# One preparation per step, shared operand forms and a wide reciprocal in the first of two attentions

## The chip, the core and the metric

The kernel runs on one core of a Trainium2 chip. Its time is the device time in microseconds (us), the median of several runs. A profiled execution of the same program gives the trace: TensorE (PE) for matrix products, with its weight loads (PEld) listed apart, VectorE (DVE), ScalarE (ACT), GpSimd (POOL) and the queue of SyncE (SP), which issues loads.

## The reference

Two layers on `x` of 128 x 64 x 128 (batch, rows, features), each a cross attention to a context of 128 x 64 x 96 and a mixture of experts. The change lies in the first attention alone:

```python
q = (x @ wq + bq).reshape(B, Sq, H, D).transpose(0, 2, 1, 3)      # x is layer-normalised; 16 heads of 8
k = (y @ wk + bk).reshape(B, -1, H, D).transpose(0, 2, 1, 3)
v = (y @ wv + bv).reshape(B, -1, H, D).transpose(0, 2, 1, 3)
scores = jnp.einsum('bhqd,bhkd->bhqk', q, k) / jnp.sqrt(D)
attn = jax.nn.softmax(scores, axis=-1)
out = jnp.einsum('bhqk,bhkd->bhqd', attn, v)
x = x + jnp.tanh(g_xattn[0]) * (out.transpose(0, 2, 1, 3).reshape(B, Sq, E) @ wo + bo)
```

After it come the first mixture, the second attention and the second mixture, which sorts rows by expert and gathers them again.

## The kernel before

`attention_of_layer0` works on 64 tiles of 128 rows, two batches in each. Four tiles are a group (`GT`), so there are 16 groups. The phase is a software pipeline written out by hand: in step t every engine works on several tiles at once, in the order of its own `step` function, and semaphores join the engines. The loop `loop_steps` runs eight steps (two groups, `u` from 0 to 7) in each iteration.

What happens to tile n, by step:
- step n: TensorE makes the scores of all 16 heads (L663, 32 rows by 64 columns of the array at a time) in one of two pairs of PSUM banks. VectorE takes the negated maximum of each head (L412) and splits it into two bf16 parts (cast L423, difference L425). TensorE transposes the parts (L737, called R in what follows) into the bank `small`.
- step n+1: ACT has copied them to `rows` (L602). TensorE adds them to the scores (the subtraction, L673), ACT takes exponentials (L571).
- step n+2: VectorE sums them for each head (L409, `denom`), takes the reciprocal (L418, 16 elements a partition) and spreads it over the 8 places of each head (L430, 16 to 128 elements). TensorE transposes the probabilities in two halves (L690); ACT copies each half (L578).
- step n+3: TensorE transposes the spread reciprocals (L706) and multiplies probabilities and values (L719, strips of 32 columns), both into `pv`. ACT copies the product (L591, `heads_raw`), VectorE multiplies by the reciprocals (L443, called heads).
- step n+4: TensorE applies the output weights (L686, y, into the bank `small`), VectorE adds y to X (L436, the X update).

VectorE's order in a step is sum (n+2), maximum (n), reciprocal (n+2), cast and parts (n), wide copy (n+2), X update (n+4), heads (n+3). After heads come, in three of a group's four steps, the statistics of a later group (L375, L379), `offset` (L385) and `v_odd` (L393, half of the copies of values). R of step t waits, besides the parts, for the X update of the same step, since y and the transposed parts share a bank:

```python
if tile_now(t, 4) is not None:
    pe.wait_ge(x_updated, t - 3)
pe.transpose(rows_ps, parts[:], c.ident_bf[:]).then_inc(rows_mm, 1)
```

Each group also needs four preparations in the one bank `prep`, in the order KEYS, ROWS (transposes of the normalised rows, L633), QUERIES and VALUES. For group g they are made in the steps of group g-1: KEYS and ROWS in the first step, KEYS between subtraction and y, ROWS and the others behind the values product, QUERIES in the second, VALUES in the third, none in the fourth. Keys and queries are made with 64 columns of weights at a time (L638), values in the same way (L644). ACT copies the results out (`evacuate`). GpSimd multiplies `kT` by four masks (`spread_k`, L494) into one of two `k_heads`, in the second step of the group, takes the power -1/2 of the variance (L70, L72) and adds the output bias to X (L485).

## Time and profile before

| | |
|---|---|
| median of 3 runs | 909.94 us (908.78 to 912.01) |
| profiled execution | 908.92 us, its span 907.1 us, granted TensorE clock 0.959 of full |
| busy in the whole span | PE 777.2 us, PEld 600.7, DVE 690.6, ACT 568.8, POOL 469.1 |
| first attention (to about 321 us), stretch 202.00 to 238.40 | 36.40 us: PE 35.77, PEld 23.93, DVE 33.00, ACT 28.02, POOL 17.49; clock 1.00 |

Busy times are those of a profile: matmuls are pipelined and their ends are modelled, so the distance from one start to the next says more than the duration. The two numbers behind a form such as 32*64 are the rows and columns of the array that an operand uses. The records of an fp32 product are two for each matmul.

### The profile page before, as it was taken

Reading aid. Unit: us, or ns where it says so; the run is one execution under the profiler, and the core shown is the slowest. Engines: PE = TensorE matmul, PEld = TensorE weight load, DVE = VectorE, ACT = ScalarE, POOL = GpSimd, SP = SyncE. Lnnn points to the kernel's source line nnn. Section 1 sums busy time; section 2 is a strip of 40 time slices with the busy share of each in tenths; the row PEclk is TensorE's granted clock in tenths of the full one; section 3 lists DMA queues with packets and bytes.
Section 4 is the critical chain, followed back from the end, with each engine's and each line's share of the span. In section 5 each row is a group of like instructions: output and inputs, shape, how many; then the busy total and the mean of one; then the engine's idle time right before and its main releaser. Section 6 shows DMA issues by size and latency. Waiting matters only on the chain. (4 is left out here: it accounts for less than half of the span.)

```text
span 907.1 us, 26462 instructions
## 1 busy us (share of the span) xinstructions
PE 777.2 (86%) x8408; PEld 600.7 (66%) x8408; DVE 690.6 (76%) x2993; ACT 568.8 (63%) x1209; POOL 469.1 (52%) x505
## 2 busy tenths in 40 slices
PE   4999999999999889998998987876887888888870
PEld 2566666666666557676676665766787777788870
DVE  3989889888998968888887877455676565668764
ACT  3777777777777566878888775354354454455430
POOL 3554445444555012377777766645555555555560
PEclk9999999999999989999999999688899999999995
DMA  9101000010000020011111111311223322246638
GB/s 243 43 23 43 20 20 20 27 34 20 20 20 2 3 59 10 13 51 46 42 52 45 49 45 40 89 49 49 68 78 86 90 70 79 76 122 171 176 91 280
DMA packets 62329, 58.12 MB, mean 64 GB/s; under 512 B 10327, under 2 KB 52216, under 8 KB 62232
## 3 DMA queue, kind: packets, MB, share of 16 engines
q1 hardware_dynamic: 44664, 34.42, 14.3%
q0 software_dynamic: 8640, 17.84, 5.7%
q10 hardware_dynamic: 8928, 4.70, 1.8%
q8 instruction: 45, 0.74, 0.3%
q14 instruction: 52, 0.43, 0.2%
HBM read 32.91 MB, written 24.02 MB: 63 GB/s over the span
## 5 line engine op out<-in xcount | busy, mean ns | idle before, releaser
L1132 POOL DMA_INDIRECT contributions<-v_heads,d_token x142 | 137.9, 971 | 105.6 <-PE bc_bank L1882 67.9
L1863 PE MATMUL bc_bank<-d_xT,d_w 128*128 128x128 f32 x1136 | 161.6, 287 | 35.6 <-DVE d_xT L1381 30.1
L1863 PEld LDWEIGHTS bc_bank<-d_xT,d_w 128*128 128x128 f32 x1136 | 143.0, 197 | 46.1 <-DVE d_xT L1381 37.6
L1116 POOL DMA_INDIRECT sorted_rows<-r_send,r_slots x128 | 126.7, 990 | 47.3 <-issue 40.3
L1640 ACT ACTIVATE b_hidden<-bc_bank 128x256 f32<-128x256 f32 x142 | 54.5, 384 | 143.8 <-PE bc_bank L1863 126.5
L494 POOL TENSOR_SCALAR a_k_heads<-a_kT,first 128x512 f32<-128x512 f32 x60 | 93.1, 1569 | 0.8 <-ACT a_kT L547 0.8
L1634 ACT COPY d_w<-w 128x512 f32 x142 | 87.1, 614 | 4.2 <-issue 1.9
L412 DVE TENSOR_REDUCE a_neg_max<-a_scores 128x16 f32<-128x1024 f32 x64 | 78.1, 1221 | 8.1 <-PE a_scores L663 6.9
L571 ACT ACTIVATE a_probs<-a_scores 128x1024 f32<-128x1024 f32 x64 | 65.6, 1025 | 29.5 <-PE a_scores L673 29.4
L578 ACT COPY a_probsT<-a_probsT_bank 128x512 f32<-128x512 f32 x128 | 74.8, 584 | 13.4 <-PE a_probsT_bank L690 12.8
L690 PE MATMUL a_probsT_bank<-first,a_probs 128*128 128x128 f32 x512 | 79.7, 278 | 2.2 <-ACT a_probsT L578 0.3
L409 DVE TENSOR_REDUCE a_denom<-a_probs 128x16 f32<-128x1024 f32 x64 | 77.3, 1209 | 1.7 <-issue 1.3
L663 PE MATMUL a_scores<-a_k_heads,a_qT 32*64 32x256 f32 x1024 | 70.8, 391 | 3.0 <-issue 2.7
L1376 DVE TENSOR_TENSOR b_hidden<-b_hidden,bc_bank 128x256 f32<-128x256 f32 x72 | 29.9, 416 | 53.6 <-ACT b_hidden L1640 20.5
L690 PEld LDWEIGHTS a_probsT_bank<-first,a_probs 128*128 128x128 f32 x512 | 57.7, 141 | 12.5 <-issue 5.8
L485 POOL TENSOR_TENSOR X<-X,out_bias 128x512 f32 (+1 forms) x16 | 20.3, 1269 | 87.6 <-ACT a_xn L534 84.9
L1709 PE MATMUL bc_bank<-b_xnT,w 128*128 128x512 f32 x96 | 50.3, 636 | 12.8 <-ACT c_kT L1559 7.5
L1376 DVE TENSOR_TENSOR b_weighted<-b_hidden,bc_bank 128x256 f32<-128x256 f32 x70 | 29.1, 416 | 34.5 <-PE bc_bank L1882 20.2
L1873 PE MATMUL bc_bank<-first,d_rows 128*128 128x128 f32 x142 | 39.7, 279 | 11.8 <-DVE d_xT L1381 7.5
L1392 DVE TENSOR_SCALAR v_heads<-bc_bank,d_ends 128x128 f32<-128x128 f32 x142 | 48.7, 343 | 1.0 <-PE bc_bank L1882 1.0
L1760 PE MATMUL bc_bank<-w,b_weighted 128*128 128x128 f32 x384 | 46.8, 278 | 0.1
L1398 DVE COPY w_in<-w 128x256 f32 x142 | 46.5, 328 | 0.2
(213 smaller groups left out, 1894.1 us busy)
## 6 DMA issues: line engine op xcount, KB each, us to landing
d_rows<-sorted_rows SPq DMA_DIRECT2D x142, 65.0 KB
X<-in_x SPq DMA_DIRECT2D x16, 256.0 KB, 3.1
b_hidden<-contributions SPq DMA_DIRECT2D x8, 512.0 KB
b_weighted<-contributions SPq DMA_DIRECT2D x8, 512.0 KB
out_x<-X ACTq DMA_DIRECT2D x16, 256.0 KB
ctxT<-in_ctx_T SPq DMA_DIRECT2D x16, 192.0 KB, 3.0
c_ctxT<-in_ctx_T SPq DMA_DIRECT2D x16, 192.0 KB
contributions<-v_heads,d_token POOLq DMA_INDIRECT x142
```

The lines of the kernel that those rows point to most:

```text
L409: dve.reduce_sum(denom[:], probs[u % 2][:].rearrange("p (h k) -> p h k", k=S), AX_X).then_inc(sum_done, 1)
L412: dve.tensor_reduce(neg_max[:], scores[u % 2][:].rearrange("p a (h k) -> p (a h) k", k=S), AX_X, ALU.max, negate=True).then_inc(max_done, 1)
L494: last = pool.tensor_scalar(keys_of_head(par, j), kT[:], c.head_of_group[:, j:j + 1], None, ALU.mult)
L571: act.activation(probs[(u + 1) % 2][:], scores[(u + 1) % 2][:].rearrange("p a n -> p (a n)"), ACT.Exp, scale=SCALE0).then_inc(exp_done, 1)
L578: act.copy(probsT[u % 2][:, half * HU // 2:(half + 1) * HU // 2, :].rearrange("p u q -> p (u q)"), probsT_bank[:]).then_inc(pT_ev, 1)
L663: last = pe.matmul(scores[u % 2][S * b:S * b + S, s, bass.ts(h, 4 * S)], qT[par][rows_in, h, tile, :], k_heads[par][rows_in, tile, h].rear ...
L690: last = pe.transpose(probsT_bank[:, bass.ts(k, P)], probs[u % 2][:, bass.ts(half * HU // 2 + k, P)], c.ident[:])
L1116: pool.indirect_dma_start(dispatch.rows, bass.IndirectOffsetOnAxis(ap=slots[n % 2][:, k, j:j + 1], axis=0), send[n % 2][k][:, j, :], None) ...
L1132: pool.indirect_dma_start(dispatch.contributions, bass.IndirectOffsetOnAxis(ap=token[:, t % KEEP:t % KEEP + 1], axis=0), shares[t % KEEP], ...
L1376: dve.tensor_tensor(d_hidden[m % 4].rearrange("p k n -> p (k n)"), silu[m % 2], uv[m % 2][:, KH * P:2 * KH * P], ALU.mult).then_inc(h_read ...
L1634: act.copy(w12[t % 3][:], c.w12[:, bass.ds(experts[t % 4], 1)].rearrange("d a i h -> d (a i h)")).then_inc(w12_ready, 1)
L1863: last = pe.matmul(uv[m % 2][:, bass.ts(i, P)], w12[m % 3][:, bass.ts(i, P)], xT[m % 4][:], start=True, stop=True)
```

## The change

The diff does four things.
- Operand forms: keys, queries and values are made with strips of 32 columns, four at a time, and the subtraction in pieces of 64 columns.
- Preparations: KEYS goes to the fourth step of a group (`PREP_AT`), for the group after the next one, behind the values product; `preparations` lists them for TensorE and ACT. In step 0 the keys of group 1 are made as well.
- GpSimd: the four masks are spread over three steps (`SPREAD_AT`), the bias is added a step earlier and for a group nearer, behind the first mask, and `later_zeros` is issued in step 62.
- VectorE: L418 is gone; at the place of L430 stands one reciprocal with 128 results a partition, which reads `denom` spread over 8 places. The semaphore `rec_done` goes with it.

```diff
@@ -300,7 +300,6 @@
     probs = [sb(f"a_probs{i}", [P, H * S], F32) for i in range(2)]
     probsT = [sb(f"a_probsT{i}", [P, HU, P], F32) for i in range(2)]
     denom = sb("a_denom", [P, H], F32)
-    rec = sb("a_rec", [P, H], F32)
     wide_rec = [sb(f"a_wide_rec{i}", [P, H, DH], F32) for i in range(2)]
     heads_raw = sb("a_heads_raw", [P, P], F32)
     heads_outT = sb("a_heads_outT", [P, P], F32)
@@ -320,7 +319,7 @@
     prep_mm, prep_ev, v_odd_ev = sem("a_prep_mm"), sem("a_prep_ev"), sem("a_v_odd_ev")
     k_heads_ready = sem("a_k_heads")
     scores_mm, max_done, part1_done, parts_ready = sem("a_scores_mm"), sem("a_max"), sem("a_part1"), sem("a_parts")
-    sum_done, rec_done, raw_ready = sem("a_sum"), sem("a_rec_done"), sem("a_raw_ready")
+    sum_done, raw_ready = sem("a_sum"), sem("a_raw_ready")
     wide_rec_ready = sem("a_wide_rec")
     rows_mm, rows_ready, sub_mm, exp_done = sem("a_rows_mm"), sem("a_rows_ready"), sem("a_sub_mm"), sem("a_exp")
     pT_mm, pT_ev = sem("a_pT_mm"), sem("a_pT_ev")
@@ -328,8 +327,9 @@
     y_mm, x_updated = sem("a_y_mm"), sem("a_x_updated")
     PREP = 4
     KEYS, ROWS, QUERIES, VALUES = range(PREP)
-    PREP_AT = ((ROWS,), (QUERIES,), (VALUES,), ())
+    PREP_AT = ((ROWS,), (QUERIES,), (VALUES,), (KEYS,))
     NORMALISE_AT = ((), (0,), (1,), (2, 3))
+    SPREAD_AT = ((0,), (1, 2), (3,), ())
     LAST = TILES + 4
 
     def keys_of_head(par, j):
@@ -348,6 +348,12 @@
     def group_at(g0, more):
 
         return None if static(g0) and g0 + more >= G else g0 + more
+
+    def preparations(t, u, g0):
+
+        first = [(1, KEYS)] if static(t) and t == 0 else []
+        parts = first + [(2 if k == KEYS else 1, k) for k in PREP_AT[u % GT]]
+        return [(group_at(g0, more), (u // GT + more) % 2, k) for more, k in parts if group_at(g0, more) is not None]
 
     with nc.Block() as block:
         @block.sync
@@ -405,17 +411,12 @@
                 if m is not None:
                     dve.wait_ge(exp_done, m + 1)
                     if not static(m) or m >= 1:
-                        dve.wait_ge(rec_done, m)
+                        dve.wait_ge(wide_rec_ready, m)
                     dve.reduce_sum(denom[:], probs[u % 2][:].rearrange("p (h k) -> p h k", k=S), AX_X).then_inc(sum_done, 1)
                 if n is not None:
                     dve.wait_ge(scores_mm, n + 1)
                     dve.tensor_reduce(neg_max[:], scores[u % 2][:].rearrange("p a (h k) -> p (a h) k", k=S), AX_X,
                                       ALU.max, negate=True).then_inc(max_done, 1)
-                if m is not None:
-                    dve.wait_ge(sum_done, m + 1)
-                    if not static(m) or m >= 1:
-                        dve.wait_ge(wide_rec_ready, m)
-                    dve.reciprocal(rec[:], denom[:]).then_inc(rec_done, 1)
                 if n is not None:
                     if not static(n) or n >= 1:
                         dve.wait_ge(rows_mm, n)
@@ -426,8 +427,8 @@
                 if m is not None:
                     if not static(m) or m >= 2:
                         dve.wait_ge(spread_mm, m - 1)
-                    dve.wait_ge(rec_done, m + 1)
-                    dve.tensor_copy(wide_rec[u % 2][:], rec[:].unsqueeze(2).broadcast_to([P, H, DH])).then_inc(wide_rec_ready, 1)
+                    dve.wait_ge(sum_done, m + 1)
+                    dve.reciprocal(wide_rec[u % 2][:], denom[:].unsqueeze(2).broadcast_to([P, H, DH])).then_inc(wide_rec_ready, 1)
                 w = tile_now(t, 4)
                 if w is not None:
                     if u % GT == 0:
@@ -485,26 +486,30 @@
                 pool.tensor_tensor(X[:, bass.ts(g, GT), :], X[:, bass.ts(g, GT), :],
                                    c.out_bias0[:].unsqueeze(1).broadcast_to([P, GT, D]), ALU.add).then_inc(bias_added, 1)
 
-            def spread_k(g, par):
-
-                wait_alone(pool, prep_ev, PREP * g + KEYS + 1)
-                if not static(g) or g >= 2:
-                    wait_alone(pool, scores_mm, GT * (g - 1))
-                for j in range(4):
+            def spread_k(g, par, heads):
+
+                if heads[0] == 0:
+                    wait_alone(pool, prep_ev, PREP * g + KEYS + 1)
+                    if not static(g) or g >= 2:
+                        wait_alone(pool, scores_mm, GT * (g - 1))
+                for j in heads:
                     last = pool.tensor_scalar(keys_of_head(par, j), kT[:],
                                               c.head_of_group[:, j:j + 1], None, ALU.mult)
-                last.then_inc(k_heads_ready, 1)
+                if heads[-1] == 3:
+                    last.then_inc(k_heads_ready, 1)
 
             def step(t, u, g0):
+                if static(t) and t == TILES - 2:
+                    later_zeros(pool, c, dispatch)
                 if u % GT == 0:
                     g = group_at(g0, 2)
                     if g is not None:
                         deviation(g)
-                if u % GT == 1:
+                g = group_at(g0, 1)
+                if g is not None and SPREAD_AT[u % GT]:
+                    spread_k(g, (u // GT + 1) % 2, SPREAD_AT[u % GT])
+                if u % GT == 0 and not (static(t) and t < GT):
                     g = group_at(g0, 1)
-                    if g is not None:
-                        spread_k(g, (u // GT + 1) % 2)
-                    g = group_at(g0, 2)
                     if g is not None:
                         add_bias(g)
 
@@ -519,7 +524,6 @@
             add_bias(0)
             add_bias(1)
             loop_steps(pool, 2 * GT, TILES // (2 * GT) - 2, LAST, step)
-            later_zeros(pool, c, dispatch)
             c.ln.deviation(pool, 0)
             c.ln.offset(pool, 0)
 
@@ -578,9 +582,6 @@
                     act.copy(probsT[u % 2][:, half * HU // 2:(half + 1) * HU // 2, :].rearrange("p u q -> p (u q)"),
                              probsT_bank[:]).then_inc(pT_ev, 1)
 
-                g = group_at(g0, 1)
-                if u % GT == 0 and g is not None:
-                    evacuate(g, (u // GT + 1) % 2, KEYS)
                 if tile_now(t, 2) is not None:
                     keep_transposed(t - 2, 0)
                 n = tile_now(t, 3)
@@ -589,10 +590,8 @@
                     if not static(n) or n >= 1:
                         act.wait_ge(o_ready, n)
                     act.copy(heads_raw[:], pv[:, 0]).then_inc(raw_ready, 1)
-                g = group_at(g0, 1)
-                if g is not None:
-                    for k in PREP_AT[u % GT]:
-                        evacuate(g, (u // GT + 1) % 2, k)
+                for g, par, k in preparations(t, u, g0):
+                    evacuate(g, par, k)
                 if tile_now(t, 2) is not None:
                     keep_transposed(t - 2, 1)
                 if tile_now(t, 0) is not None:
@@ -634,14 +633,16 @@
                 if k in (KEYS, QUERIES):
                     w, src = (c.wk0, ctxT[par]) if k == KEYS else (c.wq0, xnT)
                     for h in range(2):
-                        for odd in range(2):
-                            last = pe.matmul(prep[S * odd:S * odd + S, bass.ts(h, GW // 2)], w[:, bass.ts(h, D // 2)],
+                        for strip in range(4):
+                            odd, s = strip // 2, strip % 2
+                            last = pe.matmul(prep[bass.ts(strip, STRIP), bass.ts(h, GW // 2)], w[:, bass.ts(2 * h + s, STRIP)],
                                              src[:].rearrange("p (t b q) -> p b t q", b=2, q=S)[:, odd],
                                              start=True, stop=True)
                 if k == VALUES:
                     for b in range(GB):
-                        for odd in range(2):
-                            last = pe.matmul(prep[S * odd:S * odd + S, bass.ts(b, D // 2)], ctxT[par][:, bass.ts(b, S)],
+                        for strip in range(4):
+                            odd, s = strip // 2, strip % 2
+                            last = pe.matmul(prep[bass.ts(strip, STRIP), bass.ts(b, D // 2)], ctxT[par][:, bass.ts(2 * b + s, STRIP)],
                                              c.wv0[:].rearrange("p (u h w) -> p h u w", h=2, w=DH)[:, odd],
                                              start=True, stop=True)
                 last.then_inc(prep_mm, 1)
@@ -670,12 +671,10 @@
 
                     pe.wait_ge(rows_ready, n + 1)
                     for s in range(2):
-                        last = pe.matmul(scores[(u + 1) % 2][:, s, :], rows[bass.ts(s, STRIP), :], c.head_cols[bass.ts(s, STRIP), :],
-                                         start=False, stop=True, skip_group_check=True)
+                        for b in range(2):
+                            last = pe.matmul(scores[(u + 1) % 2][bass.ts(b, S), s, :], rows[bass.ts(s, STRIP), bass.ts(b, S)],
+                                             c.head_cols[bass.ts(s, STRIP), :], start=False, stop=True, skip_group_check=True)
                     last.then_inc(sub_mm, 1)
-                g = group_at(g0, 1)
-                if u % GT == 0 and g is not None:
-                    prepare(g, (u // GT + 1) % 2, KEYS)
                 n = tile_now(t, 4)
                 if n is not None:
                     pe.wait_ge(o_ready, n + 1)
@@ -720,10 +719,8 @@
                                                  probsT[(u + 1) % 2][:, k, bass.ts(b, S)], start=(odd == 0 and b == 0),
                                                  stop=(odd == 1), skip_group_check=True)
                     last.then_inc(pv_mm, 1)
-                g = group_at(g0, 1)
-                if g is not None:
-                    for k in PREP_AT[u % GT]:
-                        prepare(g, (u // GT + 1) % 2, k)
+                for g, par, k in preparations(t, u, g0):
+                    prepare(g, par, k)
                 n = tile_now(t, 2)
                 if n is not None:
                     pe.wait_ge(pT_ev, 2 * n + 1)
```

## Rows read from the trace of the kernel before

**Rows 1.** Timeline of DVE, the maxima: start us, us, engine, line
```profile
203.45 1.22 DVE L412 TENSOR_REDUCE a_neg_max<-a_scores 128x16 f32<-128x1024 f32 x1 [0.34 <-PE a_scores L663]
...
213.30 1.21 DVE L412 TENSOR_REDUCE a_neg_max<-a_scores 128x16 f32<-128x1024 f32 x1
...
218.20 1.23 DVE L412 TENSOR_REDUCE a_neg_max<-a_scores 128x16 f32<-128x1024 f32 x1
...
221.70 1.23 DVE L412 TENSOR_REDUCE a_neg_max<-a_scores 128x16 f32<-128x1024 f32 x1
...
227.54 1.21 DVE L412 TENSOR_REDUCE a_neg_max<-a_scores 128x16 f32<-128x1024 f32 x1
...
231.40 1.21 DVE L412 TENSOR_REDUCE a_neg_max<-a_scores 128x16 f32<-128x1024 f32 x1
...
240.26 1.23 DVE L412 TENSOR_REDUCE a_neg_max<-a_scores 128x16 f32<-128x1024 f32 x1 [0.34 <-PE a_scores L663]
```

**Rows 2.** Timeline of PE, a step with keys and rows
```profile
165.48 1.09 PE L663 MATMUL a_scores<-a_k_heads,a_qT 32*64 32x256 f32 x16 [0.48 <-issue]
166.51 0.39 PE L673 MATMUL a_scores<-head_cols,a_rows 32*128 32x512 bf16 x2
166.83 1.08 PE L638 MATMUL a_prep<-ctxT,wkv 96*64 96x256 f32 x8
167.84 0.49 PE L686 MATMUL a_small<-wo,a_heads_outT 128*128 128x128 f32 x2
...
169.39 0.66 PE L633 MATMUL a_prep<-first,a_xn 128*128 128x128 f32 x4
169.88 0.60 PE L690 MATMUL a_probsT_bank<-first,a_probs 128*128 128x128 f32 x4
...
170.47 1.09 PE L663 MATMUL a_scores<-a_k_heads,a_qT 32*64 32x256 f32 x16
```

**Rows 3.** Timeline of DVE and PE, the fourth step of a group
```profile
219.34 0.24 DVE L418 RECIPROCAL a_rec<-a_denom 128x16 f32<-128x16 f32 x1
219.52 0.17 DVE L423 CAST parts<-a_neg_max 128x16 bf16<-128x16 f32 x1
...
219.73 0.17 DVE L425 TENSOR_TENSOR parts<-a_neg_max,parts 128x16 bf16<-128x16 f32 x1
219.83 0.22 DVE L430 COPY a_wide_rec<-a_rec 128x128 f32<-128x128 f32 x1
219.96 0.28 DVE L436 TENSOR_TENSOR X<-a_small,X 128x128 f32 x1
220.16 0.28 DVE L443 TENSOR_TENSOR a_heads_outT<-a_heads_raw,a_pv 128x128 f32<-128x128 f32 x1
220.36 1.21 DVE L409 TENSOR_REDUCE a_denom<-a_probs 128x16 f32<-128x1024 f32 x1
...
220.39 0.22 PE L737 MATMUL a_small<-ident_bf,parts 128*128 128x128 bf16 x1
220.54 1.09 PE L663 MATMUL a_scores<-a_k_heads,a_qT 32*64 32x256 f32 x16
```

**Rows 4.** Timeline of DVE, single operations of the third and first steps
```profile
214.81 0.55 DVE L425 TENSOR_TENSOR parts<-a_neg_max,parts 128x16 bf16<-128x16 f32 x1
...
216.15 0.77 DVE L393 COPY v_heads<-a_prep 64x256 f32<-64x256 f32 x2 [0.25 <-PE a_prep L644]
...
224.94 0.29 DVE L443 TENSOR_TENSOR a_heads_outT<-a_heads_raw,a_pv 128x128 f32<-128x128 f32 x1 [0.80 <-ACT a_heads_raw L591]
```

**Rows 5.** Timeline of POOL, the four masks of one group
```profile
209.99 6.22 POOL L494 TENSOR_SCALAR a_k_heads<-a_kT,first 128x512 f32<-128x512 f32 x4
```

**Rows 6.** Instructions by line: count, ns min/median/max, first and last start, forms
```profile
L212 DVE RECIPROCAL one_over_temp<-temp x1: 157/157/157, 311.4 to 311.4; 128x1 f32<-128x1 f32 x1
...
L1165 DVE RECIPROCAL c_rec<-bc_pair x16: 169/182/183, 361.5 to 610.9; 128x4 f32<-128x4 f32 x16
...
L418 DVE RECIPROCAL a_rec<-a_denom x64: 235/242/253, 31.5 to 316.5; 128x16 f32<-128x16 f32 x64
```

## The prediction

> **What bounds the kernel now.** The page gives TensorE (PE) the most busy time, and in the first attention its records stand end to end, so I read the order of time and not the shares. First I took the starts of VectorE's maximum (L412), one for each of the 64 tiles, which cut this phase into steps [rows 1]. Eight steps take 36.81 us (203.45 to 240.26), so a group of four takes 18.4; the four kinds of step take 4.90, 3.50, 5.84 and 3.86 us. They differ, so each must be asked for its own last wait.
>
> TensorE's own list for the step that prepares keys and rows [rows 2] gives start-to-start times: scores 1.03, subtraction (L673) 0.32, keys 1.01, from y to the end of the values product 1.55, row transposes 0.49, second transposes with the maxima's transpose (R, L737) 0.59: 4.99 us with nothing waited for. Two things are to be seen. Row transposes, four at 128 columns, take 0.49, some 0.11 us each when others follow in one form. The keys' eight records of 256 columns, two side by side in the array, should then take 8 x 0.22 / 2 = 0.87, and take 1.01: about 0.15 us goes at a change of operand form. And TensorE alone needs about 3.5 us for a step without preparation (4.99 less 1.01 and 0.49), 4.5 with the 1.01, and 17.5 for a group, if queries and values cost as much as keys.
>
> The step of 3.50 us shows the other loop [rows 1, 3]. Call the start of the maximum M. The reciprocal (L418) starts at M+1.14, cast at +1.32, parts at +1.53, the wide copy (L430) at +1.63, the X update (L436) at +1.76 and ends at +2.04. R starts 0.15 after that (220.39): it shares the bank `small` with y and waits for `x_updated`. Scores start 0.15 later, and the next maximum 1.16 after them: 2.04 + 0.15 + 0.15 + 1.16 = 3.50, the step to the hundredth. This step is bound by VectorE's small operations between the maximum and X, not by TensorE's 3.49 us of work. Had TensorE been free, VectorE's own order would need 1.96 to heads (L443), 0.20, and 1.13 for the sum (L409): 3.29. The steps of 3.86 and 4.90 are VectorE's too: there come `offset`, or `v_odd` [rows 4], plus collisions with GpSimd's work (the 0.55 us of L425 in rows 4 against 0.17 in rows 3).
>
> Only the step of 5.84 hangs on TensorE: heads (224.94) waited 0.80 us for ACT's copy of `pv` [rows 4], because keys' 1.01 us stands ahead of the values product. Heads start at M+3.24 there instead of M+1.96, and all that follows on VectorE is late by as much.
>
> **TensorE's part of the change.** Scores and subtraction share a form afterwards (32 rows by 64 columns), and so do the values product and each preparation (32-column strips). The preparations have twice the records, four side by side instead of two: the array time stays 0.87. Before, a group changes form 23 times (five in each step and one more each for keys, queries and values); afterwards 16. Seven at 0.15 is 1.05 us, 17 us over 16 groups, if TensorE were what ends last. It then needs 3.35 us for a bare step and 4.2 with a preparation, 16.5 for a group.
>
> **Keys a step ahead.** Keys' matmuls leave the step that is late on `pv` and go behind the values product of the step before. Heads there no longer wait; the 0.80 us goes, up to where VectorE's own order is late (next part). ACT's two copies of keys (L547) move along, to a step with no other evacuation. GpSimd spreads one, two and one heads in three steps and not four at once, and the bias comes a step earlier, between them: the same operations, so the same time on GpSimd, which idles between groups. Keys for the group after next are copied into `kT` only when the spread before them is over. Four heads take 6.2 us [rows 5]; they start in the statistics step, and three steps lie between it and that copy, so even with the bias among them I see no new wait. The DMA loads keep their trigger (values of two groups earlier). `later_zeros` runs straight behind the last spread in either order.
>
> **The wide reciprocal.** L418 on 16 elements and L430 on 128 go; one reciprocal of 128 elements stands at L430's place, between parts and X, which is inside the 3.50 us loop. Its duration D is in no row. Reciprocals took 157 ns for 1 element, a median of 182 for 4 (read from PSUM) and 242 for 16 [rows 6]. That is 5.7 ns an element from 1 to 16, 5.0 from 4 to 16, 8.3 from 1 to 4. Other operations grow far less: cast of 16 elements 0.17, X of 128 elements 0.28, some 1 ns each [rows 3]. Bounds: if 112 more elements streamed at 1 ns, D = 0.242 + 0.11 = 0.35; at 8.3 ns, 0.242 + 0.93 = 1.17. I take the widest span of rows, rounded down a little towards 4 to 16: 5.4 ns, D = 0.85 us.
>
> The Trainium skill, "VectorE: DVE Perf Modes", says that a reciprocal runs as an iterative divide with a repeat count of 8 at 0.96 GHz. Read as 8 cycles an element this is an estimate of 8.3 ns and D = 1.17, and the kernel would end near 942. By this reading 16 elements alone would take 133 of the 242 ns, and the trace speaks against it: that leaves 109 for the rest, where one element takes 157 in all. The duration after decides.
>
> Now M to X. L418 was also a filler: cast needs the maximum, over at M+1.23, and an operation that waits for its predecessor starts 0.04 after its end (parts after cast). So cast moves only from +1.32 to +1.27. Parts +1.48, reciprocal +1.58, X at D less the 0.09 of overlap that L430 shows, +2.34. X was at +1.76: **0.58 us later**.
>
> **The sum, per group.**
> - Plain step: 3.50 becomes 2.34 + 0.28 + 0.15 + 0.15 + 1.16 = 4.08: +0.58. TensorE has slack in it: keys now stand there, but 4.2 is reckoned from its scores, which start early when the `v_odd` step before has delayed only VectorE.
> - `offset` step: on VectorE throughout: +0.58.
> - `v_odd` step: +0.58, less the 0.25 that it waited for values [rows 4], now done in time: +0.33.
> - Statistics step: heads at M+2.54 in place of M+3.24 (`pv` is copied by about M+2.1): -0.70.
>
> Together +0.79 us a group, of 18.4. Fifteen full periods give 11.9 us; start and tail I leave even. The profiled execution took 908.9 us (span 907.1), the median is 909.9: 1.0 apart. So 920.8 against the profiled execution, 921.8, say **922**, against the median. The 17 us saved on TensorE turns into waiting for X.
>
> **Rivals.**
> - *The reciprocal streams* (D near 0.35). Then VectorE needs about the old 3.3 to 3.5 and TensorE ends last: some 17.1 us a group with the waits that remain, 1.3 less, 21 us: 889. The balance tips at D = 0.85 - 0.79/4 = 0.65 us. Below it the kernel is faster. For: doing many elements is what such an engine does cheaply. Against: three rows that rise far more than 1 ns an element. Chance 0.16.
> - *The reciprocal is steeper* (D 0.95 to 1.17): each 0.1 us is 64 x 0.1 = 6.4 us, so 928 to 942. For: the step from 1 to 4. Chance 0.10.
> - *Fewer collisions with GpSimd.* With the spread cut in three and the wide copy gone, the delayed operations (0.38 for L425 in the `v_odd` step, as much around `offset`) may fall between GpSimd's. At most 0.7 a group, 11 us: 911, no change. Against: GpSimd is busy for as long, in the same two steps, and L425 and the cast stay. Chance 0.12.
> - *As summed*: 0.62, with its own range 915 to 928.
>
> **Chances and range.** From 907 to 912.6 (0.3%, which is about what these runs can tell: their own spread is 908.8 to 912.0) nothing would be seen. Slower: the forecast and the steeper case, 0.72. Same: 0.11. Faster: the streaming case and a remnant, 0.17. The range 903 to 935 leaves out the ends at 889 and 942, about 2 in 10.
>
> **What the profile after would show.** A RECIPROCAL writing `a_wide_rec`, 128x128, at 0.85 us (right from 0.80 to 0.90). X starting 2.3 us after the maximum. The plain step at 4.1, the statistics step near 5.2. R waiting for X in most steps and TensorE's busy share in this phase falling. Preparations about 0.87 after the values product, without the 0.15 between. No wait of heads for `pv`. I would be wrong above all through D; next, if R did not wait for X, since then VectorE's sum alone holds (3.87 a plain step) and the loss shrinks by 0.2 us in one step of four.

## The result and the profile after

The changed kernel takes 928.83 us (median of 4 runs, 923.44 to 930.28), the kernel before 909.54 (4 runs, 908.78 to 912.01). The ratio is 1.0196, with a 95% interval of 1.015 to 1.0243: slower by about 2%, 17.8 us by the ratio and 19.3 us between the medians. The forecast was 922, slower, in a range of 903 to 935. Direction and mechanism held; the size was 12 us forecast against 18 by the ratio.

The profiled execution of the changed kernel took 923.4 us, the fastest of the four; its span is 921.6 against 907.1. Two starts cut the span well: the last X update began at 320.2 before and begins at 337.6 now. So the first attention lost 17.4 us, and all behind it took 2.9 us less in this execution (the other three runs, up to 930.3, were not profiled, so what varies there stays open). Inside the first attention, by the starts of the maxima: until the 9th 1.8 us (55.94 to 57.77), in six iterations of the loop 8.0, in the last seven steps 5.9, from the last maximum to the last X update 1.6.

The plain step, the fourth of a group, which took 3.50 us before [rows 1, 3], stands like this in the timeline of VectorE and TensorE of the changed kernel (start us, us, engine, line):

```profile
225.25 1.22 DVE L418 TENSOR_REDUCE a_neg_max<-a_scores 128x16 f32<-128x1024 f32 x1
226.57 0.17 DVE L424 CAST parts<-a_neg_max 128x16 bf16<-128x16 f32 x1
226.78 0.17 DVE L426 TENSOR_TENSOR parts<-a_neg_max,parts 128x16 bf16<-128x16 f32 x1
226.88 0.94 DVE L431 RECIPROCAL a_wide_rec<-a_denom 128x128 f32<-128x128 f32 x1
227.74 0.23 DVE L437 TENSOR_TENSOR X<-a_small,X 128x128 f32 x1
227.88 0.27 DVE L444 TENSOR_TENSOR a_heads_outT<-a_heads_raw,a_pv 128x128 f32<-128x128 f32 x1
228.08 1.21 DVE L415 TENSOR_REDUCE a_denom<-a_probs 128x16 f32<-128x1024 f32 x1
228.11 0.22 PE L734 MATMUL a_small<-ident_bf,parts 128*128 128x128 bf16 x1 [0.49 <-DVE X L437]
...
229.42 1.23 DVE L418 TENSOR_REDUCE a_neg_max<-a_scores 128x16 f32<-128x1024 f32 x1
```

From the maximum to the start of X it is 2.49 us, where it was 1.76; the transpose R (now L734) waits 0.49 us for X by name; 1.68 us after the start of X comes the next maximum. Sum 4.17. In the whole first attention R waits for X in 46 of 64 steps, 26.5 us together. The reciprocal takes 0.946 us in the median. Its row among the instructions by line, to be set beside [rows 6]:

```profile
L431 DVE RECIPROCAL a_wide_rec<-a_denom x64: 937/946/954, 31.9 to 332.7; 128x128 f32<-128x128 f32 x64
```

Busy time in a stretch of one iteration's length (us, then each engine with its number of instructions, the granted clock, DMA share and GB/s) shows the bound moving. TensorE was busy 35.8 of 36.4 us before; here it is 34.8 of 38.2, and VectorE 35.9:

```profile
170.80:209.00 38.20, 34.80 (x712) 23.92 (x712) 35.90 (x79) 28.62 (x63) 17.40 (x14) 1.00 0.08 24
```

In the statistics step, heads no longer wait for `pv` (first line, 2.72 us after a maximum at 210.56, where [rows 4] had 3.24), and in the values step the difference of the parts is short again (second line, 0.55 in [rows 4]):

```profile
213.28 0.27 DVE L444 TENSOR_TENSOR a_heads_outT<-a_heads_raw,a_pv 128x128 f32<-128x128 f32 x1
...
221.79 0.17 DVE L426 TENSOR_TENSOR parts<-a_neg_max,parts 128x16 bf16<-128x16 f32 x1
```

The largest single loss was not in the forecast. Between the 58th and the 59th maximum one cast of 16 elements took 4.15 us, and ended 0.04 us after GpSimd's zeros did. This is the timeline of the changed kernel there:

```profile
291.05 1.23 DVE L418 TENSOR_REDUCE a_neg_max<-a_scores 128x16 f32<-128x1024 f32 x1
292.38 4.15 DVE L424 CAST parts<-a_neg_max 128x16 bf16<-128x16 f32 x1
292.47 0.52 POOL L196 MEMSET probs<- 128x512 f32 x1
...
293.14 3.35 POOL L200 MEMSET fill<- 128x3900 f32 x1
296.56 0.17 DVE L426 TENSOR_TENSOR parts<-a_neg_max,parts 128x16 bf16<-128x16 f32 x1
```

TensorE waited 3.70 us for the X update behind it, and its granted clock was then 0.50 from 298 to 300 us and 0.65 from 300 to 302; in the kernel before it was 1.00 from 24 to 320 us. Before, cast and memset met more luckily: the memset came first and the cast waited only for its rest, 1.71 us.

```profile
285.92 3.37 POOL L200 MEMSET fill<- 128x3900 f32 x1
...
287.60 1.71 DVE L423 CAST parts<-a_neg_max 128x16 bf16<-128x16 f32 x1
```

### The profile page after: what moved, and what is told of

Read it like the earlier page. It is cut to its first block and busy times, and to the rows that moved or that the text cites. A ratio compares the mean times of both kernels' runs of the same rounds, so it can differ in the third digit from the quotient of the medians.

```text
span 921.6 us, 28115 instructions
## 1 busy us (share of the span) xinstructions
PE 767.3 (83%) x9304; PEld 597.9 (65%) x9304; DVE 720.0 (78%) x2929; ACT 570.4 (62%) x1209; POOL 469.2 (51%) x505
## 5 line engine op out<-in xcount | busy, mean ns | idle before, releaser
L575 ACT ACTIVATE a_probs<-a_scores 128x1024 f32<-128x1024 f32 x64 | 65.7, 1026 | 39.5 <-PE a_scores L675 39.5
L418 DVE TENSOR_REDUCE a_neg_max<-a_scores 128x16 f32<-128x1024 f32 x64 | 78.0, 1219 | 7.8 <-PE a_scores L664 5.8
L70 POOL TENSOR_SCALAR a_rstd<-a_stats 128x4 f32<-128x4 f32 x16 | 3.7, 233 | 142.2 <-DVE a_stats L385 142.2
L431 DVE RECIPROCAL a_wide_rec<-a_denom 128x128 f32<-128x128 f32 x64 | 60.6, 946 | 0.2
L1395 DVE COPY w_in<-w 128x256 f32 x142 | 48.4, 341 | 0.5 <-issue 0.4
```

What stands on the lines that cost most here:

```text
L418: dve.tensor_reduce(neg_max[:], scores[u % 2][:].rearrange("p a (h k) -> p (a h) k", k=S), AX_X, ALU.max, negate=True).then_inc(max_done, 1)
L431: dve.reciprocal(wide_rec[u % 2][:], denom[:].unsqueeze(2).broadcast_to([P, H, DH])).then_inc(wide_rec_ready, 1)
L575: act.activation(probs[(u + 1) % 2][:], scores[(u + 1) % 2][:].rearrange("p a n -> p (a n)"), ACT.Exp, scale=SCALE0).then_inc(exp_done, 1)
```

## The experiments

Each kernel was compared with runs of the kernel before on its own chip, and that kernel took 910.5, 917.2 and 915.2 us on the three chips used. So ratios are compared, not microseconds. Beside them stand two figures of each profiled execution that no later phase can touch: eight steps of the loop, from a first maximum of an iteration to the next such one (all at a granted clock of 1.00), and the start of the last X update. The second is the rougher one. It holds single stalls: near 84 us TensorE stood for about 1 us, for nothing that the profile shows, in narrow_zeros, narrow_zeros_bias3, copylate_bias3 and half_reciprocal (0.95 to 1.14 us). And in some runs the granted clock fell at the end of the phase.

| kernel | eight steps, us | last X update, us | ratio to before (95%) |
|---|---|---|---|
| before | 36.81 | 320.2 | 1 |
| changed | 38.19 | 337.6 | 1.0196 (1.015 to 1.0243) |
| narrow_again | 34.86 | 311.3 | 0.9916 (0.9893 to 0.9939) |
| wide_alone | 39.50 | 348.2 | 1.0292 (1.0238 to 1.0347) |
| late_reciprocal | 38.14 | 335.9 | 1.0194 (1.0138 to 1.0249) |
| zeros_early | 38.17 | 332.4 | 1.0127 (1.0069 to 1.0185) |
| forms_alone | 36.19 | 315.7 | 0.9974 (0.9952 to 0.9996) |
| schedule_alone | 35.50 | 317.5 | 0.9965 (0.9938 to 0.9993) |
| narrow_zeros | 34.86 | 306.1 | 0.9860 (0.9829 to 0.9891) |
| narrow_zeros_bias | 35.38 | 309.5 | 0.9915 (0.9881 to 0.9948) |
| half_reciprocal | 35.78 | 320.9 | 0.9998 (0.9971 to 1.0025) |
| narrow_zeros_copylate | 34.58 | 306.7 | 0.9830 (0.9776 to 0.9884) |
| narrow_zeros_bias3 | 34.65 | 306.4 | 0.9819 (0.9787 to 0.9852) |
| copylate_bias3 | 34.30 | 304.0 | 0.9835 (0.9786 to 0.9885) |

The theory to test: the wide reciprocal lies in the loop from maximum over X, R and scores to the next maximum and is the whole loss, while the other parts save time. The rival: the doubled records or the moved keys, masks and bias cost time too.

**1. The old VectorE operations back in the changed kernel.**

```diff
+                if m is not None:
+                    dve.wait_ge(sum_done, m + 1)
...
+                    dve.reciprocal(rec[:], denom[:]).then_inc(rec_done, 1)
...
-                    dve.reciprocal(wide_rec[u % 2][:], denom[:].unsqueeze(2).broadcast_to([P, H, DH])).then_inc(wide_rec_ready, 1)
+                    dve.tensor_copy(wide_rec[u % 2][:], rec[:].unsqueeze(2).broadcast_to([P, H, DH])).then_inc(wide_rec_ready, 1)
```

> The changed kernel with the two old VectorE operations back (reciprocal of 16, copy to 128), everything else as changed. Theory 1 (the 0.95 us reciprocal sits in the loop maximum, X update, R, scores, next maximum, and is all of the loss): a plain step needs at most 3.5 us on that loop, TensorE becomes what ends last with some 17.1 us a group instead of 19.1, so eight steps take 34 to 35 us (changed kernel 38.2, kernel before 36.8) and the time is 893 to 900 us. Rival (the loss comes from twice the records in the preparations, or from the moved keys or masks): eight steps stay above 36.8 us and the time above 910.

Measured: 902.06 us, ratio 0.9916; eight steps 34.86. The reciprocal alone is 3.33 us in eight steps and turns a gain of 0.8% into a loss of 2%. The rival falls. The time missed the 893 to 900 expected, and the steps say where: GpSimd's zeros hold an operation here too (a step of 8.13 us), and `offset` had become slow. In the timeline of this kernel `offset` begins under GpSimd's bias addition and ends with it. Under the zeros it is not the cast (0.17 us) that is held but the wide copy, and the X update, heads and the sum behind it end only when it does:

```profile
201.58 1.27 POOL L492 TENSOR_TENSOR X<-X,out_bias 128x512 f32 x1
201.70 1.17 DVE L392 SCALAR_TENSOR_TENSOR a_minus_mean<-a_stats,a_rstd 128x4 f32<-128x4 f32 x1
...
202.79 1.21 DVE L416 TENSOR_REDUCE a_denom<-a_probs 128x16 f32<-128x1024 f32 x1
...
270.14 4.57 DVE L437 COPY a_wide_rec<-a_rec 128x128 f32<-128x128 f32 x1
...
270.83 3.88 DVE L416 TENSOR_REDUCE a_denom<-a_probs 128x16 f32<-128x1024 f32 x1
271.27 3.36 POOL L200 MEMSET fill<- 128x3900 f32 x1
```

**2. The wide reciprocal alone in the kernel before.** The same edit the other way round.

```diff
-                    dve.reciprocal(rec[:], denom[:]).then_inc(rec_done, 1)
...
-                    dve.tensor_copy(wide_rec[u % 2][:], rec[:].unsqueeze(2).broadcast_to([P, H, DH])).then_inc(wide_rec_ready, 1)
+                    dve.reciprocal(wide_rec[u % 2][:], denom[:].unsqueeze(2).broadcast_to([P, H, DH])).then_inc(wide_rec_ready, 1)
```

> The kernel before with the wide reciprocal alone. Theory 1: plain, offset and values steps gain 0.6 to 0.7 us each, the statistics step nearly nothing, since there heads wait for ACT's copy of pv until 3.24 us after the maximum in any case. Eight steps take 39.5 to 40.5 us, and the time is 930 to 938: worse than the whole change. Rival: if the other parts cost time, this kernel is faster than the changed one, below 925.

Measured: 935.81 us, ratio 1.0292, worse than the whole change. Eight steps 39.50, the low end of the range expected; plain steps 4.18, the statistics steps 5.99 and 5.84 as before, since heads there wait in any case. The `offset` steps rose by 0.30 and 0.47 us and the values steps by 0.33 and 0.25, not by the 0.6 to 0.7 expected: the wide copy, which the masks had held for 0.58 us, is gone, `offset` is free in both groups (0.15 us), and in the values step the cast takes 0.40 us where the parts had taken 0.55. Three statistics steps, with their scores at 96.1, 137.2 and 257.4 us, took 7.6 to 8.4 us. They are 5.6 us longer than three of 5.99, so the comparison with the changed kernel rests on the eight steps (39.50 against 38.19) and not on the ratio. In the first of them TensorE had just waited 0.58 us, and its granted clock was 0.51, the 1.2 GHz level, from 97.6 to 101.0 (busy time and clock in stretches):

```profile
97.00:97.60 0.60, 0.60 (x8) 0.27 (x6) 0.36 (x1) 0.00 (x0) 0.60 (x1) 1.00 0.00 0
97.60:101.00 3.40, 3.40 (x19) 2.03 (x21) 2.45 (x5) 1.96 (x4) 0.50 (x1) 0.51 0.00 0
101.00:101.60 0.60, 0.60 (x34) 0.51 (x33) 0.00 (x0) 0.49 (x1) 0.00 (x0) 0.93 0.00 0
```

**3. The wide reciprocal behind heads, off the loop through X.**

```diff
+                    dve.tensor_tensor(heads_outT[:], heads_raw[:], pv[:, 1], ALU.mult).then_inc(o_ready, 1)
+                if m is not None:
...
+                    dve.reciprocal(wide_rec[u % 2][:], denom[:].unsqueeze(2).broadcast_to([P, H, DH])).then_inc(wide_rec_ready, 1)
```

(The lines moved down; they stood ahead of the X update.)

> The changed kernel with the wide reciprocal moved behind heads, out of the loop that goes through X and R, but still in VectorE's order. Theory 1: X starts 0.86 us earlier after the maximum, R no longer waits for it; the plain step falls from 4.17 to VectorE's own sum of 3.95 to 4.0 us, the other steps stay. Eight steps take 37.7 to 38.0 instead of 38.2, the time falls by 2 to 4 us. If VectorE's queue is not what bounds (a rival in which only the latency of X counts), eight steps fall to 36 us or less and the time by over 12 us.

Measured: ratio 1.0194, eight steps 38.14, against 38.19: nothing, where 37.7 to 38.0 were expected. The expected 0.2 us of the plain step did not come: it takes 4.25 us, where it took 4.17. Only the last step of an iteration fell, from 4.71 to 4.17, and the statistics and values steps rose by 0.09 to 0.15. The timeline of such a last step says why:

```profile
206.06 1.22 DVE L418 TENSOR_REDUCE a_neg_max<-a_scores 128x16 f32<-128x1024 f32 x1
...
208.12 0.94 DVE L444 RECIPROCAL a_wide_rec<-a_denom 128x128 f32<-128x128 f32 x1
...
209.09 1.22 DVE L415 TENSOR_REDUCE a_denom<-a_probs 128x16 f32<-128x1024 f32 x1
...
210.23 1.22 DVE L418 TENSOR_REDUCE a_neg_max<-a_scores 128x16 f32<-128x1024 f32 x1
```

The sum writes `denom`, which the reciprocal just ahead of it reads, so it waits for its end and starts 0.97 us after the reciprocal's start, where an overlap of 0.09 would make 0.86; in the plain step it is 1.06. VectorE's own list now needs 4.17 to 4.25 by itself. The move took the work off one limit and left it on another at the same height: the 0.95 us of the reciprocal count in this kernel at either place in VectorE's list.

**4. GpSimd's later zeros in the start of the kernel.**

```diff
-                if static(t) and t == TILES - 2:
-                    later_zeros(pool, c, dispatch)
...
             deviation(1)
+            later_zeros(pool, c, dispatch)
```

> The changed kernel with GpSimd's later zeros (probs, values, ones, fill) issued in the start of the kernel and not in step 62. Theory: in the changed kernel the cast of one step took 4.15 us (before 1.71, usually 0.17) until GpSimd's 3.35 us memset was over; without it the two steps around it take 4.4 and 5.0 instead of 9.0 and 5.6, and the time falls by 4 to 5 us. Rival: the cast waited for something else and stays long, or the memsets delay the start by as much.

Measured: ratio 1.0127, the last X update at 332.4, 5.2 us earlier than in the changed kernel; the 59th and 60th maxima follow after 4.29 and 4.99 us instead of 9.04 and 5.56, no cast is long there, and the granted clock stays at 1.00. As expected. The 5.2 us hold both the cast and what the lower clock after it cost.

**5 and 6. The operand forms alone, and the places of keys, masks and bias alone.** The second also keeps the old VectorE operations. The core of each edit:

```diff
-                        for odd in range(2):
-                            last = pe.matmul(prep[S * odd:S * odd + S, bass.ts(h, GW // 2)], w[:, bass.ts(h, D // 2)],
+                        for strip in range(4):
+                            odd, s = strip // 2, strip % 2
+                            last = pe.matmul(prep[bass.ts(strip, STRIP), bass.ts(h, GW // 2)], w[:, bass.ts(2 * h + s, STRIP)],
```

```diff
-    PREP_AT = ((ROWS,), (QUERIES,), (VALUES,), ())
+    PREP_AT = ((ROWS,), (QUERIES,), (VALUES,), (KEYS,))
+    SPREAD_AT = ((0,), (1, 2), (3,), ())
```

> The kernel before with the new operand forms alone (strips of 32 columns in the preparations, the subtraction in the form of the scores). Theory 1: only the steps in which TensorE ends last can gain, the statistics step by the 0.15 us between scores and subtraction and the values step by its wait of 0.2; the plain and offset steps stay at 3.50 and 3.86. Eight steps take 36.1 to 36.5 instead of 36.81, the time falls by 2 to 6 us. Rival (TensorE's 17 us saved are all gained): eight steps take 34.7 and the time is near 893.

> The kernel before with the new places of keys, masks and bias alone (old operand forms, the two old VectorE operations). Theory 1: the statistics step falls from 5.9 to 4.9 us, since heads no longer wait for pv; the offset step rises from 3.86 to 4.4, since offset waits for GpSimd's bias; the others hold nearly, the plain step rising to about 3.7 by the keys. Eight steps take 35.2 to 36.0, the time is 902 to 908. Rival: if the forms carry the gain of the narrow kernel (eight steps 34.86), this one stays at 36.8.

Measured: eight steps 36.19 (ratio 0.9974) and 35.50 (0.9965), both in their ranges. Against 36.81 that is 0.62 and 1.31 us, and the two together, in narrow_again, gave 1.95: they add up. Forms gain only in the two steps where TensorE ends last or delays VectorE, statistics and values (0.12 to 0.22 us). schedule_alone shows the statistics step at 4.97 and 4.83 instead of 5.99 and 5.84, the values step at 4.33 and 4.31 instead of 4.90 and 4.98, and the offset step at 4.43 instead of 3.86 and 3.69 (the bias above it). The plain step is at 4.09 instead of 3.50, more than the 3.7 expected: keys in the old form stand in it, and the next maximum waits 0.72 us for its scores. With the new forms it is 3.59.

**7. narrow_again with the zeros early.** Edit 4 on edit 1.

> narrow_again with the later zeros in the start of the kernel. The cast of 4 us in the 59th step goes; the time falls by 4 to 6 us, to 896 to 898. Eight steps in the loop stay at 34.9.

Measured: ratio 0.9860 against 0.9916, last X update 306.1 against 311.3, eight steps 34.86 as before. As expected, by the ratio.

**8. The same with GpSimd's order of the kernel before.** All four heads of the keys are spread in one step, and the bias comes behind them.

```diff
-                g = group_at(g0, 1)
-                if g is not None and SPREAD_AT[u % GT]:
-                    spread_k(g, (u // GT + 1) % 2, SPREAD_AT[u % GT])
-                if u % GT == 0 and not (static(t) and t < GT):
+                if u % GT == 1:
                     g = group_at(g0, 1)
+                    if g is not None:
+                        spread_k(g, (u // GT + 1) % 2)
+                    g = group_at(g0, 2)
                     if g is not None:
                         add_bias(g)
```

> narrow_zeros with GpSimd's masks and bias in the order of the kernel before (four masks in the second step, then the bias, which waits for the normalised rows). Theory: offset took 1.17 to 1.23 us in narrow_again because it began under the bias addition and waited for its end; with masks there instead it takes 0.6 and the offset step falls from 4.43 to 3.9, 1.0 us in eight steps, unless TensorE's 4.2 us for a step with queries ends last there, which leaves half of it. Eight steps take 34.0 to 34.5, the time falls by 3 to 6 us. Rival: TensorE already ends last and nothing moves.

A miss: eight steps rose from 34.86 to 35.38. `offset` did fall (step 3.85 and 3.68 instead of 4.43), but the values step rose from 4.32 to 4.68 and 4.84, since the masks now hold the parts in it (0.55 and 0.63 us instead of 0.17), and the plain step from 3.60 to 3.81. And the bias now runs at the start of a group and holds the cast of the statistics step, 0.80 us instead of 0.17:

```profile
215.37 0.24 DVE L425 RECIPROCAL a_rec<-a_denom 128x16 f32<-128x16 f32 x1
215.55 0.80 DVE L430 CAST parts<-a_neg_max 128x16 bf16<-128x16 f32 x1
...
216.38 0.18 DVE L432 TENSOR_TENSOR parts<-a_neg_max,parts 128x16 bf16<-128x16 f32 x1
```

**9. Half the results in the reciprocal of the changed kernel.** Four of the eight places of each head keep the value one: this kernel leaves half of the reciprocals out, and its result is not that of the reference.

```diff
-                    dve.reciprocal(wide_rec[u % 2][:], denom[:].unsqueeze(2).broadcast_to([P, H, DH])).then_inc(wide_rec_ready, 1)
+                    dve.reciprocal(wide_rec[u % 2][:, :, 0:DH // 2], denom[:].unsqueeze(2).broadcast_to([P, H, DH // 2])).then_inc(wide_rec_ready, 1)
```

> The changed kernel, but the reciprocal makes 64 results a partition and not 128: four of the eight places of each head are left at one, so half of the reciprocals are left out. Theory 1 (duration linear in the results, 6.3 ns each between 16 and 128, and balance with the kernel before near 0.65 us): it takes 0.54 us, the plain step falls from 4.17 to about 3.8, eight steps from 38.2 to 35.2 to 36.0, below the 36.8 of the kernel before, and the time to 903 to 910. Rival (a fixed price of the spread operand and not of the number of results): the reciprocal stays above 0.7 us and eight steps above 36.8.

The reciprocal took 0.546 us, its row:

```profile
L431 DVE RECIPROCAL a_wide_rec<-a_denom x64: 540/546/553, 32.1 to 316.1; 128x64 f32<-128x64 f32 x64
```

From 16 to 64 results 6.3 ns each, (546 - 242) / 48, and from 64 to 128 6.3, (946 - 546) / 64: the price is one of results, not of the spread operand. Eight steps took 35.78 and the plain step 3.77, as expected; 35.78 is below the 36.81 of the kernel before. The whole time did not follow: ratio 0.9998. The loop's gain of 1.03 in eight steps is eaten at the end, where the cast meets the zeros again (a step of 9.08 us) and the granted clock is 0.50 from 282 to 288 us behind it: the last maximum starts at 306.57, that of the kernel before at 306.59.

**10 to 12. On narrow_zeros: the copy behind the X update, the bias behind the last mask, and both.**

```diff
                     dve.tensor_tensor(X[:, w, :], y, X[:, w, :], ALU.add).then_inc(x_updated, 1)
+                if m is not None:
...
+                    dve.tensor_copy(wide_rec[u % 2][:], rec[:].unsqueeze(2).broadcast_to([P, H, DH])).then_inc(wide_rec_ready, 1)
```

```diff
-                if u % GT == 0 and not (static(t) and t < GT):
+                if u % GT == 2 and not (static(t) and t < GT):
```

> narrow_zeros with the copy to 128 places moved behind the X update. X starts 0.13 us earlier after the maximum. Theory 1: where X, R and scores end last this gains 0.1 a step, where TensorE or the sum ends last nothing. Eight steps take 34.3 to 34.8 instead of 34.86, the time falls by 0 to 4 us.

> narrow_zeros with GpSimd's bias behind the last mask, in the third step of a group. Theory: offset, which waited in the second step for the end of the bias addition under it (1.17 to 1.23 us), takes 0.6 or less, and the second step falls from 4.43 to 3.9; the bias meets VectorE's reductions and v_odd, which are not held. Eight steps take 34.0 to 34.5. Rival: the bias holds the next small operation instead and nothing is gained, as when it stood at the start of the group.

> Both of the last two edits. Eight steps take 33.6 to 34.3 and the time is the lowest so far, 890 to 900, if each gains by itself; if TensorE with its 16.5 us a group ends last already, nothing is added to the better of the two.

Measured: eight steps 34.58, 34.65 and 34.30. The first is in its range. The second lies 0.15 above its own: `offset` is down to 0.59 and 0.16 us in turn, but the masks now hold the small operations around it, and the third step rose from 4.32 to 4.68 and 4.83:

```profile
216.95 1.21 DVE L419 TENSOR_REDUCE a_neg_max<-a_scores 128x16 f32<-128x1024 f32 x1
...
218.57 0.59 DVE L437 COPY a_wide_rec<-a_rec 128x128 f32<-128x128 f32 x1
...
219.11 0.16 DVE L392 SCALAR_TENSOR_TENSOR a_minus_mean<-a_stats,a_rstd 128x4 f32<-128x4 f32 x1
...
222.22 0.63 DVE L432 TENSOR_TENSOR parts<-a_neg_max,parts 128x16 bf16<-128x16 f32 x1
```

Together they are the best loop, the end of the range expected. In the whole time the three and narrow_zeros (ratios 0.982 to 0.986) can't be told apart. One reason is on record: from the last maximum to the last X update the two kernels with the bias in the third step took 15.0 and 15.6 us, the other two 13.5 and 13.2, and in copylate_bias3 the granted clock was 0.50 from 298 to 312 us. All four beat both kernels: 1.4 to 1.8% less than the kernel before, and by the ratios about 3.5% less than the changed one.

## Why the prediction came out as it did

**The loop through X and R: right.** Forecast for the plain step 4.08 us, measured 4.17. Three things make the difference: D 0.10 longer, the cast at +1.32 and not +1.27 (the wait for the maximum costs 0.05 more than I took), X itself 0.05 shorter. R waits for X by name. Experiments 1 and 2 show the reciprocal to be the whole loss, in either surrounding. My four kinds of step were read from two different groups: 4.90, 3.50, 5.84 and 3.86 add up to 18.10 and not to the 18.4 of a group. The other group's are 4.98, 4.05, 5.99 and 3.69, and the 4.05 is the last step of an iteration, where TensorE stands still for 0.48 us before its scores. That step rose by 0.66, about as forecast.

**The size of D: the term that was too small.** 0.85 us taken, 0.946 measured. The three rows gave 5.0 to 8.3 ns an element; I rounded towards the lower ones, and 6.3 was right. The slope over the whole span of rows, 5.7, would have been the better choice and still too low (D of 0.88). The Trainium skill, "VectorE: DVE Perf Modes", gives a repeat count of 8 (section "First, the fixed hardware budget") and a clock of 0.96 GHz ("Specifications"), which I had read as 8.3 ns, an estimate; the trace disagrees with that reading. 64 tiles times 0.096 us are 6.1 us, about what lies between 922 and 928.8, but that nearness is chance: inside the six iterations the loss was 8.0 us, where my terms gave 9.5. The first attention lost 17.4 us where my sum had 11.9, and all of that excess lies outside the loop.

**The statistics step: right.** Forecast 5.14 (5.84 less 0.70), measured 5.20, and 5.28 in the other group, where it was 5.99. Heads no longer wait for `pv`.

**The offset step: right in one group, by two errors.** Forecast 4.44, measured 4.43: D was longer, but the wide copy is gone, which the masks had held for 0.58 us. In the other group the step was 3.69 and rose to 4.44, by 0.75 and not 0.58: `offset` had been free there (0.16 us) and now waits for the bias (0.57).

**The values step: better than forecast.** 5.23 forecast, 4.98 measured. The part L426 takes 0.17 us where it took 0.55 [rows 4]: the collisions with GpSimd went from this step. The rival that named them had the right place, but 0.4 us in a group is less than the 0.7 it allowed. For eight steps my terms gave 38.39, against 38.19 measured: the sum of the loop came out well by luck, with the longer D hidden by the missing collisions.

**"Start and tail I leave even": wrong, and the largest miss of place.** Outside the six iterations the profile shows 9.3 us, where my sum had about 2.4 (fifteen periods at 0.79, less twelve in the loop). The step that failed is to take the tail as even because `later_zeros` runs straight behind the last spread in either order. It does, but what VectorE does at that moment had changed, and the cast waited 4.15 us instead of 1.71. Behind it the granted clock was at 0.50 for a while. Experiment 4 takes 5.2 us out of the changed kernel; how much the kernel before pays for its own 1.71 us was not tried. Of the rest, 2.2 us lie in the last four steps before the last maximum, which took 4.17 us each where they had taken 3.50 to 3.66: such steps pay for D, and no statistics step among them gives anything back, so a tail is not even. How much of all this reaches the median stays open, since what follows the first attention took 2.9 us less in the profiled execution.

**TensorE's saving: right that it would not show, but too large.** With VectorE relieved, it does show: 1.95 us in eight steps, of which the forms gave 0.62 and the places of keys, masks and bias 1.31. I had taken 0.15 us for each change of form, 2.1 us in eight steps. The rows of the changed kernel give less: from scores to y it is 1.23 us, where it was 1.34, and from the values product to the second transposes 1.51, 1.45 and 1.48 in the steps with keys, queries and values, where 1.60, 1.60 and 1.67 were taken with the old forms. That adds up to about 1.7 us in eight steps, an estimate from these rows. A good third of it arrived, since TensorE ends last only in some steps.

**The balance point** (D of 0.65 us): in the loop it holds roughly. At 0.55 eight steps are 1.0 us below the kernel before, at 0.95 they are 1.4 above; a straight line between gives about 0.72, an estimate. For the whole kernel the balance is near 0.55 (ratio 0.9971 to 1.0025), because of the end.

## What to carry to other kernels

Before an operation is widened to save another, price it by its number of results from rows of at least two sizes; a reciprocal at 6.3 ns a result is dear to make eight times over, when a copy of the same 128 results costs 0.22 us. When several edits come in one change, the good ones may be hidden by one bad one: here two gained 0.8% together, and the third alone lost 2.9%. A bulk memset on GpSimd belongs where no cast or copy of a critical loop can meet it: moving it was worth 5.2 us of the first attention in both surroundings (experiments 4 and 7). And each step in a pipeline has its own last wait, so a saving is worth what its steps can take and no more.

## What the runs showed of the hardware that I had not expected

Some small VectorE operations do not get through while GpSimd's operation is under way: a cast 1.71 and 4.15 us and a wide copy 4.57 us under memsets, `offset` 1.17 us under the bias addition, against 0.17, 0.22 and 0.16 us when free; each ends 0.02 to 0.08 us after GpSimd's. Maxima, bn_stats and reciprocals held their length (1.19 to 1.23, 0.27 to 0.30, 0.94 to 0.95 us) wherever GpSimd stood. So did the sums (1.18 to 1.22), but for one of 3.88 us in narrow_again and one of 3.77 in schedule_alone, which stand right behind a held copy and end with it. The Trainium skill says it ("SBUF — State Buffer", section "SBUF: two separate sides"): the port pair that VectorE and GpSimd share is an exclusive lock, which goes for the whole instruction to whichever starts first, a GpSimd operation or a VectorE operation in a two-port mode or, against a GpSimd operation that reads SBUF, with two inputs in SBUF, and the other blocks. The ends above agree. Two things go beyond it. The cast at 292.38 began before any of the four memsets, under the last mask, which ends near 292.5, and let all four go first. And under a mask the difference of the parts got through before the mask was over: in the kernel before it ends at 215.36, while the mask runs from 214.62 to 216.21, and in narrow_zeros_bias3 at 222.85, with a mask from 222.14 to 223.70. Why is open.

TensorE's clock fell to its lower level (granted clock 0.51 to 0.54 from 97.6 to 101.0, from 138.3 to 142.0 and from 258.0 to 262.0) at three of the group starts of wide_alone, in the middle of a phase in which TensorE was busy 0.92 of the time (36.2 of 39.5 us from 178.3 on). Ahead of the three, TensorE had waited 0.89 to 0.90 us for X and then stood 0.58, 0.49 and 0.53 us before its scores, for nothing that the profile shows. At the group starts near 178 and 218 us the second wait is 0.48 us (the first 0.89 again), and the clock stays at 1.00. What decides is open. The clock's other falls in this phase, in any run, came in its start or its end or, as in the changed kernel, behind the zeros.
